# Attention with routed experts on one core: new orders on all engines, first routing scores in PSUM

## What is computed

```
xn      = layernorm(x)
w       = exp(tanh(((xn @ W + b) @ xn.T) / |i - j|)), zero on the diagonal
att     = (w / (rowsum(w) + 1e-7)) @ xn
scores  = sigmoid(xn @ gate_w.T)                  # 8 experts
sel     = top 2 of scores + expert_bias
routed  = sum over sel of down_e(relu(up_e(xn * score_e))^2)   # bf16, 176 wide
shared  = down_s(relu(up_s(xn))^2)                # f32, 176 wide
out     = x + att + routed + shared
```

## Time and profile before

| what | value |
|---|---|
| median of 3 runs | 120.36 us |
| the profiled execution | 120.12 us |
| its span in the profile | 118.4 us |
| instructions | 2789 |
| matmuls | 912 |
| granted TensorE clock | 0.999 |
| moved by DMA | 16.56 MB, mean 140 GB/s |
| transposing DMAs | 31, median 3.7 us from issue to landing |
| DMA issues to store outputs | 9 |

### The profile page before, as it was taken

How to read it: one execution, slowest core, us unless ns; L and a number is a source line. 1 busy time by engine, 2 the same in 40 slices (tenths; PEclk the granted TensorE clock), 3 DMA queues, 4 the chain that set the end, 5 groups by cost and what they waited for, 6 DMA issues and landing times.

```text
span 118.4 us, 2789 instructions
## 1 busy us (share of the span) xinstructions
PE 110.9 (94%) x912; PEld 84.1 (71%) x912; DVE 99.9 (84%) x316; ACT 89.0 (75%) x138; POOL 71.5 (60%) x121
## 2 busy tenths in 40 slices
PE   3977699999999999999999999999999999999981
PEld 3934346968768786878678776869587876778780
DVE  6996889888898989989888988988988688989821
ACT  4463699798579894989689876989499867996740
POOL 6459798999993389716991499436971603215000
PEclk9999999999999999999999999999999999999999
DMA  3999306628956939296848959393938757696962
GB/s 85 302 239 312 118 0 122 122 41 169 172 111 123 176 73 208 42 214 93 154 89 200 101 108 173 78 179 81 170 77 210 130 110 134 120 213 127 158 174 89
DMA packets 47821, 16.56 MB, mean 140 GB/s; under 512 B 44992, under 2 KB 45760, under 8 KB 47808
## 3 DMA queue, kind: packets, MB, share of 16 engines
q1 hardware_dynamic: 47232, 15.44, 64.8%
q0 software_dynamic: 288, 0.72, 3.5%
q10 hardware_dynamic: 288, 0.23, 0.9%
HBM read 3.84 MB, written 2.10 MB: 50 GB/s over the span
## 4 chain that ended last, share of the span: by engine, by line
PE 86%; DVE 8%; issue 2%; ACT 1%; POOL 1%; DVEq 0%; POOLq 0%; ACTq 0%
PE out_ps L925 16%; PE h_ps L878 14%; PE side L854 11%; PE dots L833 10%; PE out_ps L913 6%; DVE gated L639 5%; PE side L867 5%; PE out_ps L907 4%; PE small L823 4%; PE out_ps L955 4%; PE small L805 4%; PE small L790 2%; PE h_ps L891 2%; PE small L814 1%; PE side L823 1%
## 5 line engine op out<-in xcount | busy, mean ns | idle before, releaser
L639 DVE SCALAR_TENSOR_TENSOR gated<-h_ps,gates 128x1408 bf16<-128x1408 f32 x28 | 45.1, 1612 | 5.0 <-PE h_ps L878 4.5
L467 ACT ACTIVATE hidden<-gated 128x1408 bf16<-128x1408 bf16 x30 | 41.3, 1376 | 2.4 <-DVE gated L654 1.2
L925 PEld LDWEIGHTS out_ps<-downT,hiddenT 128*128 128x128 bf16 x341 | 21.5, 98 | 5.7 <-issue 3.4
L925 PE MATMUL out_ps<-downT,hiddenT 128*128 128x128 bf16 x341 | 23.9, 219 | 0.0
L257 POOL TENSOR_SCALAR xn<-x_sb,meanvar,rstd 128x128 f32<-128x128 f32 x28 | 22.1, 800 | 0.8
L878 PE MATMUL h_ps<-upT,xnTb 128*128 128x512 bf16 (+1 forms) x84 | 21.3, 362 | 0.7 <-DVE gated L639 0.5
L290 POOL TENSOR_SCALAR_AFFINE_SELECT probs<-probs 128x256 f32<-128x256 f32 x16 | 6.6, 411 | 20.0 <-ACT probs L424 20.0
L833 PE MATMUL dots<-projT,xnT 128*128 128x256 f32 x60 | 15.6, 382 | 0.6 <-ACT projT L415 0.6
L854 PEld LDWEIGHTS side<-xn,probs 128*128 128x128 f32 x120 | 15.0, 191 | 1.3 <-issue 0.5
L854 PE MATMUL side<-xn,probs 128*128 128x129 f32 x120 | 15.9, 275 | 0.0
L833 PEld LDWEIGHTS dots<-projT,xnT 128*128 128x128 f32 x60 | 10.7, 190 | 4.5 <-ACT projT L415 2.3
(11 more groups left out here) (105 smaller groups left out, 171.7 us busy)
## 6 DMA issues: line engine op xcount, KB each, us to landing
x_sb<-in_x SPq DMA_DIRECT2D x7, 256.0 KB, 8.8
out_y<-final SPq DMA_DIRECT2D x7, 256.0 KB, 4.1
hiddenT<-hidden SPq DMA_TRANSPOSE x31, 3.7
upT<-in_up POOLq DMA_DIRECT2D x1, 352.0 KB, 7.2
downT<-in_down POOLq DMA_DIRECT2D x1, 352.0 KB, 8.1
out_y<-final SPq DMA_DIRECT2D x2, 128.0 KB, 1.7
late_sb<-in_late SPq DMA_DIRECT2D x1, 192.0 KB, 5.6
x_sb<-in_x ACTq DMA_DIRECT2D x1, 128.0 KB, 2.8
```

The costliest lines, as they stand in the source:

```text
L467: a.activation(hidden[:, t, :], gated[:, t, :], ACT.Square).then_inc(squared, 1)
L639: v.scalar_tensor_tensor(out=gated[:, t, :].rearrange("p (e h) -> p e h", e=E), in0=h_ps[:, 0:NH].rearrange("p (e h) -> p e h", e=E), scal ...
L925: last = t_.matmul(out_at(t), hiddenT[:, c % 2, t, j, :], downT[:, j, :], start=(t == 0 and j == 0 and c < LAST), stop=((t >= 2 or c == LA ...
```

## The change

Four of the kernel's lists are reordered: TensorE, VectorE, ScalarE and GpSimd in the part for the first chunks, which now reaches through k = 2 written out; in the loop, which now begins at k = 3; TensorE, VectorE and ScalarE also in the last chunk. SyncE's list stays as it is. No operation is added or removed. Chunk 0's routing scores are written to and read from the first 32 columns of the PSUM bank `out_ps` instead of the SBUF tensor `scores`; for this `route_scores(0)` waits for `decay_copied`, `shared_main(0)`, which writes that bank, waits for `gates_ready`, and the wait for `early_loaded` moves into `take_proj(0)`. Indentation is cut by eight columns.

```diff
@@ -176,6 +176,11 @@
 def out_at(t):
     return out_bank(t // 2)[:, (t % 2) * P:(t % 2 + 1) * P]

+def scores_at(c):
+    if c > 0:
+        return scores[:, :, :]
+    return out_ps[:, 0:TILES * E].rearrange("p (t e) -> p t e", t=TILES)
+
 def turn_at(part):
     return h_ps[:, part * CH:(part + 1) * CH].bitcast(BF16)

@@ -329,39 +334,56 @@
     normalize_fourth()
     narrow(0)
     rsqrt(1)
-    normalize(1)
+    normalize(1, 0, 1)
+    normalize(1, 1, 2)
+    normalize(1, 2, 3)
+    normalize(1, 3, 4)
+    rsqrt(2)
+    normalize(2, 0, 1)
     mask(0, 0)
+    normalize(2, 1, 2)
+    normalize(2, 2, 3)
+    normalize(2, 3, 4)
     narrow(1)
     square_rest(0)
-    rsqrt(2)
-    normalize(2, 0, 2)
     mask(0, 1)
-    normalize(2, 2, 4)
+    square_shared(0)
+    square_rest(1)
+    mask(1, 0)
     make_gates(1)
-    square_rest(1)
-    square_shared(0)
-    mask(1, 0)
+    square_first_chunk_end()
+    add_second_x()
+    mask(1, 1)
+    rsqrt(3)
+    normalize(3)
     add_x(0)
-    add_second_x()
-    square_first_chunk_end()
-    mask(1, 1)
     narrow_ident()
     narrow(2)
-    for k in range(2, NCH + 1):
+    make_gates(2)
+    mask(2, 0)
+    square_shared(1)
+    narrow(3)
+    square_rest(2)
+    add_x(1)
+    mask(2, 1)
+    for k in range(3, NCH + 1):
         f, c = k, k - 1
         if k + 1 < NCH:
             rsqrt(k + 1)
+        if k + 1 < NCH:
             normalize(k + 1)
-        if f < NCH:
-            square_rest(f)
-        add_x(c)
         square_shared(c)
         if f < NCH:
             make_gates(f)
+        if f < NCH:
+            square_rest(f)
+        if f < NCH:
             mask(f, 0)
+        if f < NCH:
             mask(f, 1)
         if k + 1 < NCH:
             narrow(k + 1)
+        add_x(c)

 @block.scalar
 def _(act):
@@ -410,6 +432,8 @@
         a.activation(pair[:, :, 0:2], top8[:, :, 0:2], ACT.Copy).then_inc(pair_set, 1)

     def take_proj(c):
+        if c == 0:
+            act.wait_ge(early_loaded, 16)
         act.wait_ge(proj_made, c + 1)
         wait(act, dots_made, Q * (c - 1))
         a.activation(projT[:, c % 2, :], proj_bank(c)[:, :], ACT.Identity, bias=b_sb).then_inc(proj_taken, 1)
@@ -469,55 +493,66 @@
     root()
     take_xT(0)
     copy_decay()
+    relu_rest(0)
     exp_logits(0)
-    act.wait_ge(early_loaded, 16)
     take_proj(0)
     take_pair(0)
-    relu_rest(0)
     take_tanh(0, 0)
     take_exp(0, 0)
     take_xT(1)
+    square(0, 0)
+    relu_rest(1)
     exp_logits(1)
-    relu_rest(1)
-    square(0, 0)
     take_proj(1)
     take_tanh(0, 1)
+    square(0, 1)
     take_exp(0, 1)
+    relu_shared(0)
+    take_tanh(1, 0)
     take_pair(1)
-    relu_shared(0)
-    square(0, 1)
-    take_tanh(1, 0)
+    scale_attention(0)
     take_exp(1, 0)
-    scale_attention(0)
-    scale_second()
     square(0, 2)
     take_xT(2)
+    scale_second()
     take_tanh(1, 1)
-    take_exp(1, 1)
     exp_logits(2)
     relu_rest(2)
-    for k in range(2, NCH):
+    take_exp(1, 1)
+    scale_attention(1)
+    square(1, 0)
+    take_proj(2)
+    square(1, 1)
+    take_pair(2)
+    square(1, 2)
+    take_tanh(2, 0)
+    take_exp(2, 0)
+    relu_shared(1)
+    square(1, 3)
+    take_xT(3)
+    take_tanh(2, 1)
+    take_exp(2, 1)
+    for k in range(3, NCH):
         f, c = k, k - 1
+        relu_rest(f)
+        exp_logits(f)
         scale_attention(c)
-        if f >= 3:
-            exp_logits(f)
-            relu_rest(f)
         square(c, 0)
         square(c, 1)
+        take_proj(f)
         take_pair(f)
-        take_proj(f)
         relu_shared(c)
         square(c, 2)
         take_tanh(f, 0)
         take_exp(f, 0)
+        square(c, 3)
         if f + 1 < NCH:
             take_xT(f + 1)
-        square(c, 3)
         take_tanh(f, 1)
         take_exp(f, 1)
     relu_shared(LAST)
+    scale_attention(LAST)
     square(LAST, 0)
-    scale_attention(LAST)
     square(LAST, 1)
     square(LAST, 2)
     square_last()
@@ -588,7 +623,9 @@
     def route_scores(c):
         dve.wait_ge(expT_taken, c + 1)
         wait(dve, gates_ready, c)
-        v.reciprocal(scores[:, :, :], onep[:, :, :]).then_inc(topk_step, 1)
+        if c == 0:
+            dve.wait_ge(decay_copied, 1)
+        v.reciprocal(scores_at(c), onep[:, :, :]).then_inc(topk_step, 1)

     def route_bias(c):
         if c == 0:
@@ -597,7 +634,7 @@
         bias = ebias.rearrange("p (a e) -> p a e", a=1).to_broadcast([P, TILES, E])
         if c == 0:
             dve.wait_ge(fillers_set, 2)
-        v.tensor_tensor(biased[:, :, 0:E], scores[:, :, :], bias, ALU.add).then_inc(topk_step, 1)
+        v.tensor_tensor(biased[:, :, 0:E], scores_at(c), bias, ALU.add).then_inc(topk_step, 1)

     def route_top(c):
         then(c, 2)
@@ -615,7 +652,7 @@

     def route_gates_first():
         dve.wait_ge(marks_set, 1)
-        v.scalar_tensor_tensor(out=gates[:, 0, :, :], in0=marked[:, :, 0:E], scalar=MARK, in1=scores[:, :, :],
+        v.scalar_tensor_tensor(out=gates[:, 0, :, :], in0=marked[:, :, 0:E], scalar=MARK, in1=scores_at(0),
                                op0=ALU.is_equal, op1=ALU.mult).then_inc(gates_ready, 1)

     def weigh(c, q):
@@ -714,56 +751,75 @@
     gate(0, 1)
     route_one(1)
     route_scores(1)
+    gate(0, 2)
     route_bias(1)
-    route_top(1)
-    gate(0, 2)
-    route_mark(1)
     weigh(1, 0)
     attend_sums(0, 0)
+    route_top(1)
     attend_norm(0, 0)
+    gate(0, 3)
+    route_mark(1)
     attend_sums(0, 1)
+    weigh(1, 1)
     attend_norm(0, 1)
-    gate(0, 3)
-    weigh(1, 1)
-    for k in range(2, NCH):
+    gate(1, 0)
+    attend_sums(1, 0)
+    attend_norm(1, 0)
+    norm_stats(3)
+    route_one(2)
+    route_scores(2)
+    gate(1, 1)
+    route_bias(2)
+    attend_sums(1, 1)
+    attend_norm(1, 1)
+    route_top(2)
+    attend(1)
+    gate(1, 2)
+    weigh(2, 0)
+    route_mark(2)
+    finish(0, 0)
+    gate(1, 3)
+    finish(0, 1)
+    weigh(2, 1)
+    for k in range(3, NCH):
         f, c, o, g = k, k - 1, k - 2, k + 1
         gate(c, 0)
         attend_sums(c, 0)
-        attend_norm(c, 0)
         if g < NCH:
             norm_stats(g)
+        attend_norm(c, 0)
         gate(c, 1)
+        route_one(f)
         finish(o, 0)
-        route_one(f)
+        route_scores(f)
         attend_sums(c, 1)
-        route_scores(f)
+        route_bias(f)
         attend_norm(c, 1)
-        route_bias(f)
         attend(c)
         route_top(f)
         gate(c, 2)
+        weigh(f, 0)
         route_mark(f)
-        weigh(f, 0)
         gate(c, 3)
+        weigh(f, 1)
         finish(o, 1)
-        weigh(f, 1)
     gate_halves(0)
     attend_sums(LAST, 0)
     attend_norm(LAST, 0)
     gate_halves(1)
+    gate_halves(2)
     finish(LAST - 1, 0)
-    gate_halves(2)
+    finish(LAST - 1, 1)
+    gate_halves(3)
     attend_sums(LAST, 1)
     attend_norm(LAST, 1)
-    finish(LAST - 1, 1)
-    gate_halves(3)
-    attend(LAST)
     at, to = PARTS[1]
     dve.wait_ge(turned, 2)
     dve.wait_ge(out_made, TILES * (LAST - 1))
     v.tensor_copy(hiddenT[:, LAST % 2, TILES - 1, at:to, :].rearrange("p j n -> p (j n)"),
                   turn_at(1)[:, 0:(to - at) * P]).then_inc(turned_taken[1], 1)
     finish(LAST, 0)
+    attend(LAST)
     finish(LAST, 1)

 @block.tensor
@@ -859,7 +915,7 @@
     def shared_main(c):
         if c == 0:
             pe.wait_ge(late_loaded, 16)
-            pe.wait_ge(decay_copied, 1)
+            pe.wait_ge(gates_ready, 1)
         if c == LAST:
             pe.wait_ge(proj_taken, c + 1)
         elif c > 0:
@@ -964,42 +1020,60 @@
     up_tile(0, 0)
     dots(0, 1)
     transpose_x(1)
+    shared_main(0)
+    up_tile(0, 1)
     rest(1)
-    up_tile(0, 1)
     project(1)
     transpose_exp(1)
-    shared_main(0)
     up_tile(0, 2)
+    dots(1, 0)
     attend(0, 0)
-    dots(1, 0)
+    transpose_x(2)
     up_tile(0, 3)
+    dots(1, 1)
     attend(0, 1)
-    dots(1, 1)
-    transpose_x(2)
     down_tile(0, 0)
-    for k in range(2, NCH):
+    up_tile(1, 0)
+    attend(1, 0)
+    down_tile(0, 1)
+    rest(2)
+    shared_down_rest(0)
+    shared_down_main(0)
+    transpose_exp(2)
+    up_tile(1, 1)
+    project(2)
+    attend(1, 1)
+    down_tile(0, 2)
+    up_tile(1, 2)
+    dots(2, 0)
+    shared_main(1)
+    transpose_x(3)
+    up_tile(1, 3)
+    dots(2, 1)
+    down_tile(0, 3)
+    down_tile(1, 0)
+    down_tile(1, 1)
+    for k in range(3, NCH):
         f, c, o = k, k - 1, k - 2
         up_tile(c, 0)
         attend(c, 0)
-        if k == 2:
-            down_tile(0, 1)
+        shared_down_rest(o)
         rest(f)
-        shared_down_rest(o)
         up_tile(c, 1)
         shared_down_main(o)
         down_tile(o, 2)
         transpose_exp(f)
         attend(c, 1)
+        project(f)
         up_tile(c, 2)
-        project(f)
-        down_tile(o, 3)
         shared_main(c)
         dots(f, 0)
+        down_tile(o, 3)
         up_tile(c, 3)
-        down_tile(c, 0)
         if f + 1 < NCH:
             transpose_x(f + 1)
         dots(f, 1)
```

(6 more changed lines are left out.)

## The result

The changed kernel takes 119.32 us (median of 13 runs, 118.58 to 120.03) beside 120.5 for the kernel before; the ratio is 0.9906, 95% interval 0.9885 to 0.9926, so about 1.1 us faster. Forecast were 118.9 us and a gain of 1.42.

The account below looks back on a forecast made before the run. The prediction took TensorE, full in the repeated step, as the bound. First chunks 0.69, rest of that part 0.00, steps 0.25 and end 0.48 sum to 1.42 us off the median: 118.9 us, range 118.2 to 120.1.

Parts of the forecast that it names:

- The step: Five repeated steps: shared_main takes 0.86 instead of 0.91 us, 0.25 us gained in all; other engines keep up.
- 0.06 for dots(7,1): Before the last chunk: dots(7,1) loses its down_tile neighbour and gets 0.06 us shorter.
- rival 1: Repeated steps: rest pays 0.20 us a step behind shared_down_rest, 1.0 in all; 119.9 us, chance 0.14.
- rival 4: Repeated steps: norm_stats ahead of attend_norm delays ScalarE, so dots waits on TensorE; slower, 121.1 us, chance 0.07.
- First chunks: Start through up_tile(1,0): TensorE's idle time is filled and up_tile(1,0) ends 0.69 us earlier.
- rival 5: More gain: the 0.46 us before gate(0,0) vanishes, or the swap gains 0.11 a step; 118.4 us, chance 0.12.
- The rest of the three-chunk part: Behind up_tile(1,0), before the repeated steps: costs and savings of the order cancel, zero within 0.04 us.
- The end: Last chunk: part 0's copy hides under down_tile(7,1), last matmul 12.99 instead of 13.41 us after up_tile(7,0); with dots 0.48.
- Tile (7,2) lands 8.2 + 3.6 = 11.8: Last chunk, us after up_tile(7,0): this tile's transposing DMA lands at 11.8, wanted at 12.22.
- the 12.3: Last chunk, us after up_tile(7,0): a last DMA landing later than 12.3 would show the prediction wrong.
- rival 3: Last chunk: the end gives nothing because a chunk 7 tile lands 0.5 us late; 119.4 us, chance 0.11.
- The bank: First chunks: putting chunk 0's scores in PSUM costs zero, bounded by 0.2 us either way.

Follow-up runs that it names:

- e2: Kernel before with the new orders in the five repeated steps alone; 120.02 us, ratio 0.9961.
- e9: Kernel before with one added line: route_scores(0) on VectorE also waits for decay_copied, long satisfied; 119.91 us, one run.
- e7: Changed kernel with ScalarE's last-chunk order as before, square(7,0) ahead of scale_attention(7); 119.16 us, ratio 0.9877 against the kernel before.
- e12: Changed kernel with down_tile(0,1) behind shared_down_rest(0) and square(7,0) ahead of scale_attention(7); 118.36 us, ratio 0.9823 against the kernel before.
- e5: Changed kernel with chunk 0's routing scores back in SBUF, all new orders kept; 119.29 us, ratio 0.9880 against the kernel before.
- e6: Kernel before with chunk 0's routing scores in PSUM and the two waits for it, old orders; 120.08 us, ratio 0.9960.
- e1: Kernel before with the new orders and the PSUM bank in the first three chunks alone; 119.92 us, ratio 0.9951.
- e4: Changed kernel with 20 warm-up matmuls of 64 columns instead of 10 of 128; 126.05 us, ratio 1.0461 against the kernel before.
- e11: The changed kernel run again, unaltered, as a yardstick; 119.36 us, ratio 0.9903 against the kernel before.
- e3: Kernel before with the new orders in the last chunk alone; 120.37 us, ratio 0.9989.
- e10: Kernel before with shared_main(0) on TensorE waiting for gates_ready instead of decay_copied, VectorE's stream unchanged; 120.52 us, one run.

## Why the prediction held, and where it did not

**The step: right.** Five steps gave 0.35 in the changed kernel, forecast 0.25 and 0.06 for dots(7,1); e2 has 0.25 in its span and 0.47 (0.23 to 0.70) by its ratio. The swap of rest and shared_down_rest costs nothing, so rival 1 is out. No step shows idle time before dots or shared_main, so rival 4, the slower one, is out: norm_stats ahead of attend_norm is taken up by the slack that was reckoned.

**First chunks: the sum held, its parts did not.** Forecast 0.69 at the end of up_tile(1,0), measured 0.98 (0.82 at its start, and 0.17 for its length: attend behind it starts 17.11 after rest(0) before, 16.13 after). Of this, 0.41 is the idle time before gate(0,0), which I let stay and had put into rival 5; without it 0.57 is left, if it counts in full (by itself, in e9, it is worth 0.32 of the span). So shared_main(0) in the gap and transpose_x(2) early gave about 0.1 less than reckoned. The trace of before could not show that a wait would do it.

**The failed step: "The rest of the three-chunk part ... zero within 0.04."** It lost 0.47: 0.29 of waiting before down_tile(0,1) and 0.18 of its length. I looked for the tightest DMA and named tile (1,1), at 5.1 us; tile (0,1) I did not check. By the changed kernel's trace it was issued at 19.4 and wanted at 24.4, so 5.0 us: 1.3 in hand at the median landing of the earlier trace rows, none at the longest. The bound that I had was right, put on one tile alone.

**The end: right order, mis-sized term.** Forecast: the last matmul visible 12.99 after up_tile(7,0). In e7 it is 12.90 (114.40 less 101.50) and in e12 the chain runs through without a wait, so copying part 0 under down_tile(7,1) does save the 0.4. In the changed kernel it came at 13.59. The step that failed is "Tile (7,2) lands 8.2 + 3.6 = 11.8": it was ready at 8.3, was issued at 9.1 and landed at 12.7, behind the 12.3 that the prediction had named as a sign of being wrong. I took the issue to follow the square, and left out the queue ahead of it; scale ahead of square(7,0), which I had costed at nothing by tile (7,0)'s own due time, made its issue 0.8 later and brought (7,0) and (7,1) within 1.5 us of each other; with this order the packet of code then fell on the start of the issue of (7,1), in six traces of six. That is rival 3, with the delay at the issue and not in the landing.

**The bank: right to be zero.** e5 and the changed kernel differ by nothing that can be measured; the Trainium skill's extra overhead on PSUM (Perfetto Trace Analysis, Optimizing Scalar/DVE Operations) does not show: route_scores(0) takes 0.36 into PSUM and 0.35 into SBUF. The bank's gain in e6 is that of its wait.

**The number: near, and in part by luck.** The median moved by 1.1 to 1.2 us, 0.2 to 0.3 less than the sum. Unforeseen were +0.41 before gate(0,0), and -0.47 and -0.6 at two DMAs. By e6's ratio the wait alone gives 0.48, the larger part of e1's 0.59, and the forecast's sum had nothing for it. Without it about 0.65 of the measured 1.13 would be left, an estimate by subtraction, and that is less than half of the 1.42.

## What to carry to other kernels

When a tuned order leaves the busiest engine no gap, list each transfer with the time from its issue to its use, and hold all of them against the longest landing in the trace, not the median: a tile that mostly needs 3.5 us needs 5.2 when a packet of code shares one of its engines. Count the queue that issues as well as the transfer: an issue that took 2.9 us instead of 1.4 held up the next, which was the one wanted last. And where a profile shows 0.5 us that nothing explains, try one satisfied wait in that engine's list before reordering; here it gave as much as the reordering of five steps (0.48 and 0.47 us by the ratios), though why it does is not known.

## What the runs showed of the hardware

- Code comes in by the same DMA engines as data: in each trace seven packets of 16 KB, 0.9 to 1.9 us each, and six of 8 KB. A transposing DMA of 0.36 MB in flight when a 16 KB packet starts takes a median 4.2 us instead of 3.6, at most 5.5; of 241 that met no packet of code, none took over 3.8. The Trainium skill (Runtime: NRT & Kernel Launch, Instruction fetch mechanics) says that code is fetched in blocks of 16 KB by the sequencer's own DMA queue and that crossing a block is mostly hidden; the size agrees with the seven packets, not with the six of 8 KB, and for the engine that runs the code it may be hidden, but here the data beside it paid 0.47 us. Which code it is, the profile doesn't say: 40 more TensorE instructions left the last packet in its place (e4).
- The issue of a transposing DMA on SyncE's queue took 1.3 to 1.7 us in the 349 cases without a 16 KB packet of code under way, about 1.6 if another was issued 1.5 us before; with one under way, 48 of 85 took 1.7 to 3.0.
- One added, satisfied wait removed 0.5 us of idle time on VectorE in all ten traces that had it (changed kernel, e1, e4 to e9, e11, e12); the four without it (kernel before, e2, e3, e10) had the idle time.
- A group of down_tile whose weights could not be loaded ahead took 0.79 of the chain instead of 0.61.
